# Attention chunks that fetch 5, 5, 5 and 4 edge columns with TensorE, and VectorE one chunk further ahead

## What is computed

```python
h = (x @ W.T).reshape(n, heads, ch)
a_s = (h * att_s[None]).sum(-1)
a_d = (h * att_d[None]).sum(-1)
logits = leaky_relu(a_s[src] + a_d[dst], neg_slope)
m = segment_max(logits, dst)
ex = exp(logits - m[dst])
alpha = ex / (segment_sum(ex, dst)[dst] + 1e-16)
out = segment_sum(alpha[:, :, None] * h[src], dst) + bias
```

## Time and profile before

| | before |
|---|---|
| median of 3 runs | 15026.58 us (15022.28 to 15072.07) |
| the profiled execution, its own time | 14966.27 us |
| its span | 14964.5 us |
| busy: PE, PEld | 12397.7 us (83%), 10572.3 us (71%) |
| busy: DVE, ACT, POOL | 8446.2 us (56%), 7971.3 us (53%), 9100.7 us (61%) |
| mean granted TensorE clock | 0.927 of full speed |
| first attention layer, first pick to end of last | 244.22 to about 3571.2 us |

### The profile page before, as it was taken

How to read it: one execution, slowest core, us unless ns; L and a number is a source line. 1 busy time by engine, 2 the same in 40 slices (tenths; PEclk the granted TensorE clock), 3 DMA queues, 4 the chain that set the end, 5 groups by cost and what they waited for, 6 DMA issues and landing times.

```text
span 14964.5 us, 207967 instructions
## 1 busy us (share of the span) xinstructions
PE 12397.7 (83%) x54859; PEld 10572.3 (71%) x54859; DVE 8446.2 (56%) x16145; ACT 7971.3 (53%) x11216; POOL 9100.7 (61%) x9606
## 2 busy tenths in 40 slices
PE   3899998995699999999299999999758888888884
PEld 2788887884588888788288878888636666666663
DVE  5555555554355555555255555555536666666665
ACT  3666666663466666666166666666434444444442
POOL 5666666666666666666666666666566556556554
PEclk9999999997799999999599999999879999999996
DMA  2333333332122222222122222222123333333332
GB/s 85 79 81 79 84 80 80 80 81 56 47 48 49 48 48 48 50 48 49 33 47 49 49 48 49 48 48 48 44 78 97 98 95 100 94 97 97 97 97 52
DMA packets 911781, 1004.21 MB, mean 67 GB/s; under 512 B 343926, under 2 KB 690196, under 8 KB 911444
## 3 DMA queue, kind: packets, MB, share of 16 engines
q1 hardware_dynamic: 575588, 753.18, 17.3%
q0 software_dynamic: 307888, 198.91, 9.1%
q10 hardware_dynamic: 28224, 51.21, 0.9%
HBM read 648.97 MB, written 353.40 MB: 67 GB/s over the span
## 4 chain that ended last, share of the span: by engine, by line
PE 71%; issue 16%; DVE 5%; another core or an unknown queue 4%; ACT 2%; POOL 1%; DMA 0%; SPq 0%; DVEq 0%; ACTq 0%; POOLq 0%
PE bank L924 56%; PE bank L921 10%; PE wide L924 2%; PE bank L961 1%; POOL nodebuf L755 1%; DVE u_sb L1702 1%; PE bank L952 1%; ACT nodebuf L1084 1%; PE wide L952 1%; DVE adf L1666 1%; DVE s_b L1692 1%; ACT oh_x L1091 1%; DVE wide L1662 0%; ACT x_nm L1001 0%
## 5 line engine op out<-in xcount | busy, mean ns | idle before, releaser
L924 PE MATMUL bank<-tab,oh 128*128 128x448 f32 x35280 | 8109.8, 375 | 870.8 <-issue 864.8
L824 POOL DMA_INDIRECT g<-table,idx x6435 | 6088.7, 946 | 3811.1 <-issue 1804.8
L924 PEld LDWEIGHTS bank<-tab,oh 128*128 128x128 f32 x35280 | 6812.7, 194 | 1781.2 <-issue 1129.2
L1091 ACT ACTIVATE oh<-nodebuf 128x896 fp32r<-128x896 bf16 x2940 | 2653.2, 943 | 3872.0 <-remote 2357.7
L1084 ACT ACTIVATE nodebuf<-nodebuf,key_at 128x640 bf16<-128x640 f16 (+1 forms) x5488 | 3890.1, 789 | 902.5 <-DMA nodebuf<-keys_m 778.1
L1575 DVE TENSOR_REDUCE g<-bank 128x32 f32<-128x480 f32 x2940 | 1812.9, 648 | 3852.6 <-remote 2537.9
L824 POOL DMA_INDIRECT g<-tablex,idx x2341 | 2208.8, 944 | 1512.9 <-issue 689.5
L921 PE MATMUL bank<-tab,oh 128*128 128x480 f32 x5880 | 1826.7, 391 | 210.1 <-issue 167.9
L924 PE MATMUL bank<-tab,oh_x 128*128 128x448 f32 x7056 | 1635.4, 379 | 160.4 <-issue 159.7
L924 PEld LDWEIGHTS bank<-tab,oh_x 128*128 128x128 f32 x7056 | 1384.4, 197 | 331.1 <-issue 196.2
L921 PEld LDWEIGHTS bank<-tab,oh 128*128 128x128 f32 x5880 | 1139.6, 194 | 345.4 <-issue 206.9
(11 more groups left out here) (300 smaller groups left out, 7575.2 us busy)
## 6 DMA issues: line engine op xcount, KB each, us to landing
state<-o_sb SPq DMA_DIRECT2D x585, 288.0 KB
g<-table,idx POOLq DMA_INDIRECT x6435
auxx<-wide SPq DMA_DIRECT2D x97, 1056.0 KB
xd_in<-auxx SPq DMA_DIRECT2D x194, 512.0 KB
nodebuf<-keys_g SPq DMA_DIRECT2D x588, 160.0 KB
nodebuf<-keys_g SPq DMA_DIRECT2D x588, 150.0 KB
xe_t<-in_edge_attr SPq DMA_DIRECT2D x196, 256.0 KB
vmax<-o_sb ACTq DMA_DIRECT2D x194, 256.0 KB
```

Of the source, the lines that this page charges most:

```text
L824: eng.indirect_dma_start(o, None, t[:, :], bass.IndirectOffsetOnAxis(ap=idx[k][:, j:j + 1], axis=0)).then_inc(e_g[k][j // (W // 2)], 16)
L924: last = eng.matmul(o[:, 0:FR], hot[:, b, at], tab[:, a, b * FR:(b + 1) * FR], start=False, stop=(b == LB - 1 and a == 1))
L1091: eng.activation(hot[:, :, at], far[:, :, at], ACT.Relu, scale=-2.0, bias=1.0).then_inc(E["oh"], 1)
```

## The change

`PICKS` goes from (5, 5, 5, 5) to (5, 5, 5, 4). The fourth chunk of each pass has four picks and twelve gathered columns. Pick c of a chunk now always uses bank c, and the helper `used` names the pick that last used slot and bank c: the one a chunk earlier, or two chunks earlier for c = 4 behind a four-pick chunk. VectorE takes the maxima of the first four chunks ahead of `fill(0)`, and in the loop takes those of the chunk three ahead where it took those of the chunk two ahead. ScalarE's one-hots and squares go to the chunks four and five ahead, and SyncE loads keys five ahead.

```diff
-PICKS = (5, 5, 5, 5)
+PICKS = (5, 5, 5, 4)
...
-assert GROUP % RING == 0 and len(PICKS) == NB
+assert SA == RING and len(PICKS) == NB
...
+def used(layer, i, k, c):
+
+    kp = max(x for x in range(k - NB, k) if PICKS[x % NB] > c)
+    return nth(layer, i - (kp < 0), kp % NB, c + 1)
...
-                for x in range(NB if step < 3 else 3):
+                for x in range(NB + 1 if step < 3 else 3):
                     if step < 3:
-                        load_sel(step, 0, x)
+                        load_sel(step, x // NB, x % NB)
...
-                    done = nth(layer, i, k, c + 1)
-                    pick(bank[(AHEAD[k] + c) % RING][:, 0:FB], oh, c, done, done - RING)
+                    pick(bank[c][:, 0:FB], oh, c, nth(layer, i, k, c + 1), used(layer, i, k, c))
...
-                        kp = (k - 1) % NB
-                        same = min(c + 1, PICKS[kp])
-                        one_hot(oh, c, i * NB + (layer * NC + k + 1), nth(layer, i - (k == 0), kp, same))
+                        one_hot(oh, c, i * NB + (layer * NC + k + 1), used(layer, i, k, c))
...
-                    if left > 3:
-                        hots(*ahead(i, k, 3))
-                    if left > 4:
-                        keys_in(*ahead(i, k, 4))
+                    if left > 4 and not (isinstance(i, int) and i + k == 0):
+                        hots(*ahead(i, k, 4))
+                    if left > 5:
+                        keys_in(*ahead(i, k, 5))
...
-                    two = (i + (k + 2) // NB, (k + 2) % NB)
+                    three = (i + (k + 3) // NB, (k + 3) % NB)
+                    more = left > 3 and not (isinstance(i, int) and i + k == 0)
                     if left > 1:
                         logits(*one)
-                    if left > 2:
-                        picked(*two, 0, 2)
+                    if more:
+                        picked(*three, 0, 2)
                     sums(i, k)
-                    if left > 2:
-                        picked(*two, 2, SA)
+                    if more:
+                        picked(*three, 2, SA)
...
                 fresh()
+                for k in range(NB):
+                    picked(0, k, 0, SA)
                 fill(0)
-                for k in range(2):
-                    picked(0, k, 0, SA)
                 logits(0, 0)
```

More of the change, by code:

```diff
@@ L644, in steps @@
                     v = i * NB + k
+                    if not isinstance(i, int) or v + 5 < NC:
+                        load_sel(layer, i + (k + 5) // NB, (k + 5) % NB)
                     if not isinstance(i, int) or i + 1 < NI:
-                        load_sel(layer, i + 1, k)
                         load_idx(layer, v + layer * NC if isinstance(v, int) else v + (layer * NC), v + NB, k)
@@ L665, in _ @@
                 four(0)
-                with eng.Fori(1, NI - 1) as i:
+                with eng.Fori(1, NI - 2) as i:
                     four(i)
+                four(NI - 2)
                 four(NI - 1)
@@ L1123, in chunk @@
                         exps(*ahead(i, k, 1))
-                    if left > 3:
-                        hots(*ahead(i, k, 3))
-                    if left > 4:
-                        keys_in(*ahead(i, k, 4))
+                    if left > 4 and not (isinstance(i, int) and i + k == 0):
+                        hots(*ahead(i, k, 4))
+                    if left > 5:
+                        keys_in(*ahead(i, k, 5))
                 halves(layer)
[L1130 to L1133, removed]
+                for x in range(NB + 1):
+                    keys_in(x // NB, x % NB)
+                    hots(x // NB, x % NB)
                 exps(0, 0)
@@ L1136, in _ @@
                     chunk(0, k)
-                with eng.Fori(1, NI - 1) as i:
+                with eng.Fori(1, NI - 2) as i:
                     for k in range(NB):
                         chunk(i, k)
-                for k in range(NB):
-                    chunk(NI - 1, k)
+                for i in (NI - 2, NI - 1):
+                    for k in range(NB):
+                        chunk(i, k)
             node(3)
@@ L1574, in picked @@
                         need(eng, E["sel"], done)
-                        v_.tensor_reduce(view(g[k], c * F, [[1, F]]), view(bank[(AHEAD[k] + c) % RING], 0, [[1, F], [F, TB]]), AX.X, ALU.max)\
+                        v_.tensor_reduce(view(g[k], c * F, [[1, F]]), view(bank[c], 0, [[1, F], [F, TB]]), AX.X, ALU.max)\
                           .then_inc(E["red"], 1)
```

## The result

| | before, on the same chip | after |
|---|---|---|
| median | 15040.31 us (15022.28 to 15072.07) | 16724.72 us (16710.86 to 16784.59) |
| span of the profiled execution | 14964.5 us | 16715.0 us |
| mean granted TensorE clock | 0.927 | 0.859 |

The ratio is 1.1125, with a 95% interval of 1.109 to 1.116. The forecast was 14,589 us; the result lies 2,136 us above it and outside its range, and beyond the rival that ended slower (15,274).

What follows compares the result with a forecast made beforehand. TensorE's own instruction stream was taken as the bound inside the layers, the other engines following. Picks −494, layer start +24, a_d +12 and layer end +20 gave −438 us: 15,027 to 14,589 us, range 14,490 to 14,700.

Steps and rivals of the forecast that it cites:

- If the bursts go with instructions, each takes its share along: 147 × 3.36 = 494.: Attention layers: TensorE's stops without semaphore waits shrink with its instructions, so 147 removed picks save 3.36 us each, 494 us.
- The lower end, 422: Attention layers: if TensorE's stops don't go with instructions, each of 147 removed picks saves only its undisturbed 2.87 us.
- 45 gathers take 55.1 us of a pass ... hidden, with 8.7 us left.: GpSimd in the loop: the 147 added gathers cost nothing, covered by 63.8 us of picks per pass; uncovered, 180 us.
- They are let go later too ... Nobody waits.: GpSimd's gathers: index loads come a chunk later, but so does reader `logits`; over ten us remain, so no cost.
- GpSimd takes over, and it ends slower.: Rival, chance 0.05: all 13.4 us of GpSimd's waiting per pass stay, a pass takes 68.5 us, total 15,274 us.
- The bursts belong to the pass or to the time.: Rival, chance 0.12: TensorE's stops don't shrink with picks; 422 us saved, 56 lost, total 14,661 us.
- The tighter slots bite.: Rival, chance 0.08: work behind the four-pick chunk takes 1 us more than it has; 147 us return, total 14,736.
- A layer's start and end.: TensorE stands about 8 us behind chunk 4 (+24 over three layers) and 6.7 us longer before `joins` (+20).
- The transfer of a_d: Layer start: a_d comes some 30 us later, its transfer beside full-rate picks; 4 us a layer, +12 in all.
- gain 0: Layer start: maxima ahead of `fill(0)` remove VectorE's wait for a_d, but TensorE waits for none of it, so no gain.
- The crawl at the start: Rival, chance 0.08: the lone, slow matmuls at each layer's start vanish, gaining 60 us more, total 14,529 us.
- The place of the bursts and the page on instruction fetch.: Loop: by the page, stops should come at the branch once in 67 us; the trace has four to five a pass.

Runs made afterwards that it cites:

- the calm machine: Not an edit: the machine of the three last jobs, where the unchanged kernel before took 12,680 us instead of 14,808 to 15,040; what sets it apart is unknown.
- the one-line edit that takes 10% back: Changed kernel with each gather waiting for TensorE's picks of its own chunk instead of the chunk before: 14,980.45 us, ratio 1.0117 to the kernel before.
- picks alone: Kernel before with picks 5, 5, 5, 4 and bank c for pick c, all leads as before: 14,993.02 us, ratio 1.013 to the kernel before.

## Why the prediction was wrong, point by point

**"If the bursts go with instructions, each takes its share along: 147 × 3.36 = 494."** This is the first step that failed. The bursts don't belong to the pick. Neither their distance (a median of 132 matmuls and weight loads before, 166 after) nor their length is TensorE's own: they end with GpSimd's pauses and are gone with the gathers. With the pace kept the kernel is 1.3% slower although a pick of each pass is gone, and even without the added gather the removed picks gave 50 us. The lower end, 422, is what they gave on the calm machine (424), where there are no bursts. Where there are, both ends were wrong, since the pick wasn't in the sum that sets the pass.

**"45 gathers take 55.1 us of a pass ... hidden, with 8.7 us left."** The second, and the larger one in what follows from it. The rows for it were there: GpSimd waits 13.4 us in a pass, and 53.9 + 13.4 is the pass. I read the waits as slack because they ended with TensorE's picks. Slack would have absorbed a gather; these don't, and by the theory they are the pauses that TensorE's instructions need. A gather costs 1.3 to 1.6 us of a pass (820 us for 588, 192 to about 240 for 147), where I had put 0.

**"They are let go later too ... Nobody waits."** The third, which makes the 11%. I asked whether the gathered rows would come in time for their reader. They do on this machine: VectorE has no wait for a gathered row between 600 and 3400 us. That was the wrong question: many of the gathers' own waits for picks became idle, and with them the pace. It shows in GpSimd's pauses, 4.92 us each in place of 2.55, and in the one-line edit that takes 10% back. On the calm machine the same move costs nothing.

**GpSimd takes over, and it ends slower.** This rival had its mechanism right in part: with all 13.4 us staying, it gave 68.5 us a pass, and with the pace kept 67.6 was measured. It had 0.05, because I counted the 135 waits that end with a matmul as slack. It missed that the waits could grow, to 22.4 us a pass. On the calm machine it came true literally, at 56.3 us a pass, for 194 us; my 63.8 for the picks of a pass had hidden it, since I compared GpSimd with a TensorE that GpSimd itself had slowed.

**The bursts belong to the pass or to the time.** Nearest in what it said of the pick, at 422 less 56. It had no place for a loss.

**The tighter slots bite.** Excluded where it can be seen: with 44 gathers the changed kernel has a window of 19 × 2.88 us a pass without a wait.

**A layer's start and end.** Right in size. The end of the first layer and TensorE's stand in the second layer's start, in the changed kernel:

```profile
4150.67 0.61 PE L892 MATMUL wide<-ident,erow 128*34 128x128 f32 x2 [18.36 <-DVE erow L1439]
...
4525.85 1.17 PE L929 MATMUL bank<-tab,oh 128*128 128x480 f32 x2 [7.98 <-DVE g L1580]
```

I had said 18.5 us ahead of `joins`, where it was 11.80, and 8 us behind chunk 4. Both were met, as terms of some 7 and 8 us a layer beside a loss of 1,684; the stand behind chunk 4 is 7.6 and 6.3 us in the first and third layer. VectorE's wait for a_d is gone in this start. The transfer of a_d, 4 us a layer, was not told apart. The "gain 0" for the maxima ahead of `fill(0)` holds only here: on the calm machine TensorE does stand behind them, for 72 us in place of 86.

**The crawl at the start** is still there: lone matmuls with up to 2.4 us between them from 4429 to 4455 us, as in the earlier trace rows. On the calm machine it is gone.

**The place of the bursts and the page on instruction fetch.** By the Trainium skill, page Runtime: NRT & Kernel Launch, section Instruction fetch mechanics, the cost of crossing a block of instructions is mostly hidden, and a taken branch to code outside the window stalls. On the calm machine the trace agrees with its first half, and has no stall even at the loop's branch (57.6 us a pass). On the other one, if the bursts are such stalls, it agrees with neither: they come 3.6 times a pass, not once, and the gathers decide whether they are hidden. I had noted the disagreement, and used it only to choose between two prices of a pick. It should have made me ask what else was going on at these moments; two rows of GpSimd's timeline beside TensorE's would have raised the question.

## What to carry to other kernels

If the busiest engine waits for "issue" in bursts, lay the other engines' timelines beside a few of these bursts before pricing a removed instruction at the engine's average rate. Waits of another engine that look like slack can be time that the busiest one needs, so a change that makes them idle, or longer, is a change to the critical path. And test the sum from the other side: if an engine's work plus its waits make the loop's length, ask what the loop becomes when that engine gets one item more. On a machine without the bursts, compare the engines at the undisturbed rates, or a new bound stays hidden behind the old slowness.

## What the runs showed of the hardware that I had not expected

- In three jobs TensorE slowed down again and again at matmuls that wait for no semaphore (a shortage of instructions, as I read it). With the pace kept half of these stretches have ended 1.8 to 2.1 us after GpSimd stops issuing indirect DMAs (medians of six kernels). With 8 gathers of 0.94 us in a pass there is not one stretch in the loop; with 44 a pass is 67.2 us instead of 57.6.
- The same program took 14,808 to 15,040 us in three jobs, and 12,680 us in three others, with a spread of 0.1% there. TensorE's "issue" waits in the loops are missing in the latter. The changed kernel is 11% slower in the one and 1.8% faster in the other. Of the kernels that keep all of the work none was found best on both: the kernel before wins where the bursts are, the changed one where they are not (picks alone, with the leads of before and all of its gathers, was not run there).
- An indirect DMA of 128 rows takes GpSimd 1.25 us from start to start, in the traces of both machines. On the calm machine 19 picks take the same time beside 8 gathers in a pass as beside 40 (12,256 and 12,254 us), as long as GpSimd's total stays under TensorE's.
